# Two layers of transformer blocks on one core: merged heads transposed by one DMA for both halves, peaks in two PSUM banks, two weight splits and one bank moved

## The reference

```python
def layer(x, ctx):                     # x (2, 1024, 256), ctx (2, 77, 192)
    h = layer_norm(x);  x = x + attention(h, h, wq1, wk1, wv1, wo1, bo1)
    h = layer_norm(x);  x = x + attention(h, ctx, wq2, wk2, wv2, wo2, bo2)
    h = layer_norm(x);  a, gate = split(h @ w_ff1 + b_ff1)
    return x + (a * gelu(gate)) @ w_ff2 + b_ff2

def attention(x, c, wq, wk, wv, wo, bo):      # 16 heads of 64
    q, k, v = heads(x @ wq), heads(c @ wk), heads(c @ wv)
    p = softmax(q @ k.T / 8)
    return merge_heads(p @ v) @ wo + bo
```

## Time and profile before

| | |
|---|---|
| median of 3 runs | 2160.64 us (2157.67 to 2160.73) |
| profiled execution: time, span | 2162.83 us, 2161.1 us |
| PE busy | 2087.5 us, 97% of the span |
| DVE, ACT, POOL busy | 75%, 68%, 64% |
| mean granted clock of PE | 0.995 of full speed |
| all waits of PE that the profile lists for L1097, L1160 and L894 on oT | 5.3, 6.4 and 4.1 us |

### The profile page before, as it was taken

How to read it: one execution, slowest core, us unless ns; L and a number is a source line. 1 busy time by engine, 2 the same in 40 slices (tenths; PEclk the granted TensorE clock), 3 DMA queues, 4 the chain that set the end, 5 groups by cost and what they waited for, 6 DMA issues and landing times.

```text
span 2161.1 us, 58920 instructions
## 1 busy us (share of the span) xinstructions
PE 2087.5 (97%) x25120; PEld 1413.0 (65%) x25120; DVE 1618.5 (75%) x3014; ACT 1473.5 (68%) x1950; POOL 1375.3 (64%) x860
## 2 busy tenths in 40 slices
PE   6999999999999999999999999999999999999999
PEld 2666666775666666668466666676746666667675
DVE  6888887657688888765768888866577888885664
ACT  4888889345488888834548888874455888886442
POOL 6878887353378887835347887773424888775540
PEclk8999999999999999999999999999999999999999
DMA  4322220040332232004032233100403323210120
GB/s 137 77 56 65 72 73 19 11 96 26 77 92 65 56 84 61 19 16 99 25 94 75 65 77 77 45 29 9 97 21 90 85 72 83 56 39 21 23 62 20
DMA packets 134245, 127.82 MB, mean 59 GB/s; under 512 B 83424, under 2 KB 95712, under 8 KB 133984
## 3 DMA queue, kind: packets, MB, share of 16 engines
q1 hardware_dynamic: 133744, 123.67, 23.0%
q10 hardware_dynamic: 240, 0.39, 0.1%
HBM read 55.72 MB, written 4.19 MB: 28 GB/s over the span
## 4 chain that ended last, share of the span: by engine, by line
PE 74%; DVE 9%; ACT 5%; POOL 4%; issue 4%; DMA 2%; SPq 1%; POOLq 1%; DVEq 0%; ACTq 0%
PE work L980 10%; PE scores L1004 9%; PE scores L997 9%; PE scores L894 5%; PE scores L896 5%; PE scores L895 5%; PE work L1026 5%; PE work L1022 5%; PE work L1024 5%; PE work L894 4%; PE work L896 4%; PE work L895 4%; DVE minima L1574 2%; ACT prob L1374 1%; PE work L1034 1%
## 5 line engine op out<-in xcount | busy, mean ns | idle before, releaser
L830 POOL TENSOR_TENSOR prob<-prob 128x1024 f16<-128x1024 f32 x328 | 709.4, 2179 | 290.1 <-ACT prob L1374 274.4
L1574 DVE TENSOR_REDUCE minima<-work 128x1 f32<-128x512 f32 x1024 | 681.7, 683 | 53.3 <-PE work L980 47.2
L1373 ACT ACTIVATE prob<-scores 128x1024 f32<-128x1024 f32 x512 | 526.3, 1028 | 94.8 <-PE scores L1004 75.1
L1374 ACT ACTIVATE prob<-scores 128x1024 f16<-128x1024 f32 x512 | 522.8, 1021 | 0.0
L1022 PE MATMUL work<-vals,prob 128*128 128x65 f16 x4096 | 428.8, 192 | 2.2 <-POOL prob L830 1.8
L1026 PE MATMUL work<-vals,prob 128*128 128x65 f16 x4096 | 429.4, 195 | 0.0
L1024 PE MATMUL work<-vals,prob 128*128 128x64 f16 x4096 | 429.2, 193 | 0.0
L1022 PEld LDWEIGHTS work<-vals,prob 128*128 128x128 f16 x4096 | 383.0, 99 | 66.1 <-issue 17.9
L1024 PEld LDWEIGHTS work<-vals,prob 128*128 128x128 f16 x4096 | 379.8, 97 | 52.8
L980 PE MATMUL work<-ka,qa 128*128 128x512 f16 x1024 | 390.2, 384 | 24.6 <-DVE minima L1574 19.2
L1026 PEld LDWEIGHTS work<-vals,prob 128*128 128x128 f16 x4096 | 380.2, 97 | 0.0
(11 more groups left out here) (168 smaller groups left out, 4161.3 us busy)
## 6 DMA issues: line engine op xcount, KB each, us to landing
qa<-staged_q SPq DMA_DIRECT2D x128, 128.0 KB, 2.3
ka<-staged_k SPq DMA_DIRECT2D x126, 128.0 KB, 2.3
raw_even<-in_pairs SPq DMA_DIRECT2D x32, 384.0 KB, 3.4
raw_odd<-in_pairs SPq DMA_DIRECT2D x32, 384.0 KB, 3.4
raw_odd<-in_pieces SPq DMA_DIRECT2D x20, 512.0 KB, 3.4
raw_even<-in_pieces SPq DMA_DIRECT2D x20, 512.0 KB, 3.5
qb<-staged_q SPq DMA_DIRECT2D x64, 128.0 KB, 2.3
kb<-staged_k SPq DMA_DIRECT2D x63, 128.0 KB, 2.3
```

Of the source, the lines that this page charges most:

```text
L830: pool.tensor_tensor(prob[1][:, slot, :], prob32[:, slot, :], prob[0][:, slot, :], ALU.subtract).then_inc(a.polished, 1)
L1373: act.activation(prob32[:, n % RING, :], source, ACT.Exp)
L1374: act.activation(prob[0][:, n % RING, :], source, ACT.Exp)\
L1574: dve.tensor_reduce(minima[:, t, h:h + 1], out[:, :], AX.X, ALU.max, negate=True)\
```

## The change

Four edits, all in the order of work or in where data stands; no matmul, exponential or subtraction is added or taken away.

1. `oT`, two tensors before, becomes one, in which both parts of a pair and half of the tokens stand side by side. The buffers already held both parts side by side, so one transposing DMA of 128 x 1024 replaces two of 128 x 512: 13 a round and not 26.
2. The later peaks take work[0] and work[2] in turn for the first ten (those beside score steps 0 to 2). The head of values that first uses work[2] (`seq == 1`) waits until the tenth has been reduced.
3. POOL's split of piece 8 moves from after `polish(3)` to before the first polish of cross attention, with a wait for the third of DVE's splits of the normalised rows; that of piece 9 moves from after `polish(6)` to after `polish(3)`. The split of the last pair's "C" weights moves from step 7 of unit 13 to step 3 of unit 14, ahead of that step's polish.
4. The last `cv` of a round takes the bank work[0], which belonged to the peaks of self attention and is free by then; the merge behind it waits only for the merge ahead of it.

```diff
@@ -118,11 +118,24 @@
     uses = [s % X_BUFFERS for s in range(X_LAID)]
-    return (g * uses.count(buffer) + uses[:until].count(buffer)) * 32
+    return (g * uses.count(buffer) + uses[:until].count(buffer)) * 16
 X_LATER_AT = {0: (2, 3), 1: (0, 1, 2, 3), 2: (0, 1, 2, 3), 3: (0, 2)}
 X_LATER_STEPS = max(X_LATER_AT)
 X_LATER = [(HALF + t, g) for t in range(HALF) for g in range(len(PEAK_GROUPS))]
+X_SHARED = sum(len(X_LATER_AT[n]) for n in range(X_LAG + 1))
+def x_turn(k):
+    later = k - PEAKS_ROUND // 2
+    return later % 2 if later < X_SHARED else 0
+def x_previous(k):
+    return max(j for j in range(PEAKS_ROUND // 2, k) if x_turn(j) == x_turn(k))
@@ -237,13 +250,16 @@
             loads[3].append(Step("bias", 0, par, 0, 0))
+        if last:
+            loads[3].append(Step("split", ("C", pair), par, 0, 0))
         if pair == 1:
             loads[0].append(Step("reload", 0, par, 0, 0))
         loads[6].append(Step("fetch", ("C", pair + 1), par, 0, 0))
     else:
         if pair + 2 <= PAIRS:
             loads[3].append(Step("split", ("S", pair + 2), par, 0, 0))
-        loads[7].append(Step("split", ("C", pair + 1), par, 0, 0))
+        if pair != PAIRS - 2:
+            loads[7].append(Step("split", ("C", pair + 1), par, 0, 0))
         if pair < 5:
@@ -305,6 +321,8 @@
+LAST_CV = max(n for n, s in enumerate(s for s in STEPS if s.kind in HIGH) if s.kind == "cv")
@@ -396,9 +414,12 @@
         x_high = work[0]
+        x_later = [x_high, work[2]]
         def high_bank(n):
+            if n == LAST_CV:
+                return self_peaks[0]
             return first_high[n] if n < len(first_high) else self_high
@@ -411,7 +432,9 @@
-            return x_early[k % len(x_early)] if k < PEAKS_ROUND // 2 else x_high
+            if k < PEAKS_ROUND // 2:
+                return x_early[k % len(x_early)]
+            return x_later[x_turn(k)]
@@ -450,7 +473,7 @@
         o_nat = sb("o_nat", [P, 2, TILES, P])
-        oT = [sb(f"oT{i}", [P, PAIRS, TOKENS], F16) for i in range(2)]
+        oT = sb("oT", [P, PAIRS, BLKS, 2, BLK], F16)
@@ -466,6 +489,15 @@
         c32 = o_nat[:, :, :, :].rearrange("p a b c -> p (a b c)")[:, 0:BATCH * 2 * CTX_COLS]
+        def oT_block(part, pair, block_):
+            return oT[:, pair, block_, part, :]
+        def oT_tile(part, c, t):
+            at = t % HALF * P
+            return oT[:, c, t // HALF, part, at:at + P]
@@ -481,14 +513,18 @@
-        def lay(s, part):
+        def lay_both(s):
             b = s % X_BUFFERS
             if b < 2:
                 home = xn[:, 2 * b:2 * b + 2, :].rearrange("p t d -> p (t d)")
             else:
                 home = t32[:, b - 2, :, :].rearrange("p c n -> p (c n)")
-            return home.bitcast(F16)[:, part * BLK:(part + 1) * BLK]
+            return home.bitcast(F16)
+        def lay(s, part):
+            return lay_both(s)[:, part * BLK:(part + 1) * BLK]
@@ -676,10 +712,8 @@
                     sp.wait_ge(xlay_low, g * X_LAID + s + 1)
-                    for part in range(2):
-                        sp.dma_start_transpose(oT[part][:, pair, block_ * BLK:(block_ + 1) * BLK]
-                                               .rearrange("p (t q) -> p t q", q=P),
-                                               lay(s, part)).then_inc(xlaid[s % X_BUFFERS], 16)
+                    sp.dma_start_transpose(oT[:, pair, block_, :, :].rearrange("p i (t q) -> p (i t) q", q=P),
+                                           lay_both(s)).then_inc(xlaid[s % X_BUFFERS], 16)
                 if g + 1 < ROUNDS:
@@ -845,6 +879,9 @@
+                hold(pool, norm_split, (g * 3 + 1) * GROUPS + 3)
+                hold(pool, y_full, g * (3 * TILES) + TILES)
+                split_piece(8)
                 for n in range(X_ALL + X_LAG):
@@ -854,10 +891,6 @@
                     elif n == 3:
-                        hold(pool, y_full, g * (3 * TILES) + TILES)
-                        split_piece(8)
-                    elif n == 6:
                         split_piece(9)
@@ -902,7 +935,12 @@
                     n = pace.here(*HIGH)
-                    if n >= len(first_high):
+                    if n == LAST_CV:
+                        pe.wait_ge(a.peak_free, pace.n(*PEAK) + PEAK_RING)
+                    elif n == LAST_CV + 1:
+                        pe.wait_ge(a.work_free, pace.n(*HIGH) - 1 + HIGH_RING)
+                    elif n >= len(first_high):
                         pe.wait_ge(a.work_free, pace.n(*HIGH) + HIGH_RING)
@@ -1081,9 +1119,9 @@
                     k = done["peak"]
-                    if k >= PEAKS_ROUND // 2:
-                        high_free()
-                    elif k >= len(x_early):
+                    if k >= PEAKS_ROUND // 2 + 2:
+                        pe.wait_ge(xpeak_free, g * PEAKS_ROUND + x_previous(k) + 1)
+                    elif len(x_early) <= k < PEAKS_ROUND // 2:
                         pe.wait_ge(xpeak_free, g * PEAKS_ROUND + k + 1 - len(x_early))
@@ -1150,6 +1188,9 @@
                             bank = x_outs[seq % len(x_outs)]
+                            if seq == 1 and starts:
+                                pe.wait_ge(xpeak_free, g * PEAKS_ROUND + PEAKS_ROUND // 2 + X_SHARED)
                             if starts and seq >= len(x_outs):
@@ -1341,7 +1382,7 @@
                         out = bank()
-                        act.activation(oT[0][:, pair, s * BLK:(s + 1) * BLK], out[:, :], ACT.Copy)\
+                        act.activation(oT_block(0, pair, s), out[:, :], ACT.Copy)\
                            .then_inc(a.work_high, 1)
...
```

More of the change, by code:

```diff
@@ L1050, in project @@
                         pe.wait_ge(a.work_free, last_merge)
-                    last = three(out, [oT[part][:, c, t * P:(t + 1) * P] for part in range(2)],
+                    last = three(out, [oT_tile(part, c, t) for part in range(2)],
                                  [wide[part][:, (w + c // 4) * PIECE + (c % 4) * DIM:
```

13 lines of the change are left out of this document (6 added, 7 removed).

## The result

The changed kernel takes 2147.69 us (median of 4 runs, 2146.43 to 2148.22) against 2159.66 us before: a ratio of 0.9944, 95% interval 0.9928 to 0.9959. That is inside the predicted range and 2.7 us above the predicted 2145. The two profiled executions stand further apart than the medians: 2162.8 us before, 2148.0 after, 14.8 us.

What follows compares the result with a forecast made beforehand. PE, busy 97% of the span, bounds the kernel, so only its waits can be won. 8.4 + 3.0 + 3.3 + 3.6 - 2.4 = 15.9 us off 2162.8, then 2.2 to the median, gave 2144.7, say 2145 us; range 2139 to 2153.

Steps and rivals of the forecast that it cites:

- Peaks in two banks: Later peaks of cross attention: all seven stalls a round go, 2.1 us a round gained, 8.4 in all, range 4 to 9.
- The rival with 1.2 us a round there: Wait ahead of the second head of values costs a whole reduction, 1.2 us a round: 2149 us, chance 0.1.
- The end of cross attention: PE's 6.4 us of waits at the last but one step's values shrink to 3.4: gain 3.0, range 1 to 3.4.
- ACT's wait goes in either case: End of cross attention: ACT's 2.65 us wait for a transposing DMA goes whether or not the two DMAs are merged.
- the slower rival: Double-size transposing DMA costs far more than two small ones; at 5 us each, 12 us a round: 2193 us, chance 0.03.
- The clock behind that wait: Output projection behind cross attention: with no wait over 0.9 us the clock does not fall, gain 3.3 us, bounds 0 and 3.3.
- 1.66 us twice: Clock falls at the output projection in rounds 0 and 3, each costing 1.66 us, both expected to go: 3.3 us.
- The threshold that the text read: Waits of PE: the clock held after 1.45 us and fell after 1.67 us.
- The late C split: POOL's C split moved into unit 14: tile 3's scores 0.45 us later in three rounds, 1.05 in round 3; 2.4 us lost.
- The rival that the clock falls there: Behind the late split in unit 14, a clock fall costs 1.66 us, four times, 6.6 us: 2151.5 us, chance 0.22.
- The last value projection: Last cv of a round: its 1.02 us wait for the merge ahead goes, gain 3.6 us in all.
- PE leaves the unit 0.9 us earlier: Unit 15: PE meets ACT again at the last score tile and leaves 0.9 us earlier, bounds 0 and 1.2.

Runs made afterwards that it cites:

- the second trace of the kernel before: The kernel before, unchanged, run and profiled once more: 2158.16 us with its profile, profiled span 2156.4 us.
- the changed kernel's second trace: Profile of the changed kernel, nothing edited, timed once more: median 2146.32 us, profiled span 2147.4 us.
- the second comparison: The changed kernel, nothing edited, timed again against the kernel before: 2146.32 us, ratio 0.9938 (0.9925 to 0.9951).
- two such swaps on DVE: Against the changed kernel, each alone: unit 15's gather ahead of the second merge's lower part, 2144.98 us; cross attention's last refine behind step 8's gather, 2144.83 us.
- the one with the later refine: The changed kernel with DVE's last refine of cross attention behind its gather of step 8, not ahead of it: 2144.83 us, ratio 0.9931.

## Why the prediction was right, and where not

- **Peaks in two banks, 8.4 forecast: right, 8.74 measured**, and 8.8 when the bank alone was taken back. The new wait ahead of the second head does not show, so the 0.1 us charged for it was too much. The rival with 1.2 us a round there is out.
- **The end of cross attention, 3.0 forecast: right, 3.6 measured** (6.83 less two falls of the clock at 1.6; against the second trace of the kernel before, which has no fall, the lead grows by 3.6 as well). The remaining wait is 0.76 where 0.85 was forecast. The reason held in the main: the splits on GpSimd made the transfer late. With the merged DMA and the old splits ACT's wait for it and 2.3 us of PE's are back; with two DMAs and the new splits PE loses 0 to 0.6. But "ACT's wait goes in either case" was wrong: with two DMAs ACT still stands 1.86 us for the transfer, and what saves PE is that ACT has this time. An issue costs 1.3 us, not the 2.0 that I took "because the work doubles with the size", but as the text said, it did not decide anything. The larger DMA lands 0.8 us later than the small one, far from the 5 us of the slower rival.
- **The clock behind that wait, 3.3 forecast: the right kind of term, taken too large.** In neither trace of the changed kernel does the clock fall at the end of cross attention, as forecast. The step that failed is "1.66 us twice": it took the two falls of one execution for those of every execution. By the mean clocks the kernel before has 1.4 falls an execution, 2.2 us, and the changed kernel gives 0.2 of that back; 2.0 us are left of 3.3. The threshold that the text read between 1.45 and 1.67 us of waiting does not exist either: the second trace holds the full clock behind 1.95 and 1.78 us, and the changed kernel's second trace loses it behind 1.53. A piece was also counted twice. The forecast took off the 2.2 us by which the profiled execution stood above the median, and by the same count about 1.0 of them, (2 - 1.4) x 1.6, are those very falls.
- **The late C split, -2.4 forecast: right in its waits, -2.15 measured**, by the steps given: a late polish, 0.45 us a round (measured 0.38) and 1.05 in round 3 (measured 1.00). The rival that the clock falls there had a chance of 0.22 and came true in part: not in all four places or in none, as it was put, but in about one of five over all traces with this split, and once in the changed kernel's nine runs.
- **The last value projection, 3.6 forecast: the mis-sized term, 1.0 measured.** The failed step is "PE leaves the unit 0.9 us earlier". The wait at `cv` went as said, and PE met ACT at the last score tile as said. I then looked for what else PE needs from ACT, and not for what it needs from DVE. The gather for value tile 4 was just in time for a PE that stood at `cv`; for the earlier PE it is 0.81 us late. What makes it late is DVE's program order: it stands behind a lower part that waits for ACT. The rows behind this list show that it could have been seen.
- **The sum.** Without the clock the four terms measure 8.74 + 3.6 + 1.0 - 2.15 = 11.2 us, and with 2.0 us for the clock 13.2. The medians gave 12.0 and, in the second comparison, 13.8 us. From the forecast: 15.9 - 2.6 (`cv`) - 1.3 (clock) + 0.3 + 0.6 + 0.3 (peaks, end, C split) = 13.2. Two terms were 3.9 us too high together, and three that were 1.2 us too low made up for a part of it; that part is luck.

What the list of waits before the change doesn't show at value tile 4 stands in the timelines of the kernel before. PE's start at 912.90 comes 0.47 us after that of the last score matmul, where 0.22 is the pace: 0.25 us of stall, for which the list has no row. The gather that it waits for already stood behind a lower part that waited for ACT:

```profile
911.51 0.69 DVE L1545 TENSOR_TENSOR oT<-work,oT 128x512 f16<-128x512 f32 x1 [1.89 <-ACT oT L1344]
...
912.33 0.42 DVE L1593 TENSOR_TENSOR o_nat<-work,inv 128x256 f32<-128x256 f32 x1
...
912.90 0.19 PE L1022 MATMUL work<-vals,prob 128*128 128x65 f16 x1
```

The Trainium skill's row that I had weighed stands in DMA: Bandwidth & Descriptors, in the section on why a DMA increments its semaphore by 16 and not by 1, and not in the one that the prediction names; it has one push for each tile of a transposing DMA in the generations before. By that the issue should grow with the size. Here it went from 1.27 to 1.31 us for twice the size; the measurement decides. The other (SBUF — State Buffer, section "SBUF: two separate sides", the exclusive lock between VectorE and GpSimd) agrees with the new rows again: the DVE refine at 884.07 takes 1.60 us beside the split, against 1.21 us for one that runs freely, and it ends 1.08 us after the split's last operation, as the refine of the earlier trace rows ended 1.08 us after the polish.

## What to carry to other kernels

When a wait is removed, follow the freed engine to the next thing that it takes from every other engine, and read in that engine's program what stands ahead of the instruction that it needs. A short instruction that frees a bank should not stand behind one that waits for a third engine: two such swaps on DVE brought 7 us here, more than the merged DMA, the moved splits and the last bank together. A fall of the clock behind a wait is an event with a chance, so before it goes into a sum, look for the same wait in other rounds and in a second profile, and count the falls over all runs by their mean clock.

## What I had not expected of the hardware

- An issue of a transposing DMA costs 1.27 us for 128x512 and 1.31 for 128x1024 elements of 2 bytes; the landing goes from 2.4 to 3.2 us after the start of the issue. So merging nearly halves the time that SP spends on issues and adds 0.8 us to the landing.
- The clock's fall isn't set by the length of the wait alone. After 1.53 us on the same semaphore in the same place it fell 7 times in 36; after 1.95 us it fell in one execution and held in another, and after 1.78 us it held. It never showed behind the waits of 0.76 us that stand at the end of cross attention now, nor behind one of 1.71 us there in the kernel with the old splits. Behind each of the two falls of the kernel before, the granted clock is at its lower level for about 3.4 us (0.60 over the 4.28 us of the earlier trace rows, an estimate from these two figures), and a fall costs 1.6. What tells the two cases apart stays open: no experiment here looked for it.
- Kernels with the same waits of 1.53 us differ in how often the clock falls: by their mean clocks once in nine runs of the changed kernel, and six times in five runs of the one with the later refine. This too is unexplained.
